# First tile list spread over a turn, the last group's routing put beside the first expert tiles, second tile list two turns later

## The reference

```python
h = h + retention(layernorm(h))              # block A: 8 heads, complex q k v, decay mask, gate
x = layernorm(h)                             # block B: softmax attention, 8 heads
t = layernorm(x + attention(x)) * g + b      # input of block C
probs = softmax(t @ gate_W + gate_b)         # block C: 8 experts, one per token
idx, gw = argmax(probs), max(probs)
out = gelu(t @ W1[idx] + b1[idx]) @ W2[idx] + b2[idx]
return h + out * gw
```

## Time and profile before

| | |
|---|---|
| median of 3 runs | 1406.74 us (1406.08 to 1408.68) |
| the profiled execution's own time | 1403.12 us |
| its span | 1401.3 us |
| TensorE busy | 1349.5 us, 96% |
| VectorE busy | 1010.8 us, 72% |
| ScalarE busy | 718.5 us, 51% |
| GpSimd busy | 407.1 us, 29% |

### The profile page before, as it was taken

The page is one execution under the profiler, slowest core; times in us unless marked ns, Lnnn a source line. Parts: engine busy times, 40 slices in busy tenths (PEclk is TensorE's granted clock), DMA queues, the critical chain, the costliest instruction groups (busy, mean ns, idle before and its releaser), DMA issues.

```text
span 1401.3 us, 40349 instructions
## 1 busy us (share of the span) xinstructions
PE 1349.5 (96%) x14878; PEld 989.6 (71%) x14879; DVE 1010.8 (72%) x2331; ACT 718.5 (51%) x1630; POOL 407.1 (29%) x268
## 2 busy tenths in 40 slices
PE   7899999999999999999999999999999876999998
PEld 5566666666666666666666666666666545899998
DVE  2677777777777777777777777777777865766665
ACT  2255555555555555555555555555555535456655
POOL 0002222222222222222222222222222224656666
PEclk9999999999999999999999999999999979899999
DMA  9322222222222222322232223222221002343332
GB/s 388 139 73 78 84 84 83 84 84 84 84 85 84 84 84 85 84 85 85 84 84 84 83 83 84 84 83 78 79 78 37 14 14 52 93 126 102 105 102 67
DMA packets 95130, 124.61 MB, mean 89 GB/s; under 512 B 56619, under 2 KB 77149, under 8 KB 94592
## 3 DMA queue, kind: packets, MB, share of 16 engines
q1 hardware_dynamic: 38400, 102.47, 22.8%
q0 software_dynamic: 56576, 19.93, 6.8%
HBM read 101.27 MB, written 20.82 MB: 87 GB/s over the span
## 4 chain that ended last, share of the span: by engine, by line
PE 90%; DVE 3%; issue 2%; DMA 2%; POOL 1%; ACT 1%; SPq 0%; DVEq 0%; POOLq 0%; ACTq 0%
PE bank_emb L427 19%; PE bank_z L415 9%; PE bank_s L486 9%; PE bank_y L500 6%; PE bank_s L725 5%; PE bank_x L415 5%; PE bank_s L415 5%; PE bank_x L592 4%; PE bank_s L552 4%; PE bank_y L415 3%; PE bank_z L574 3%; PE bank_x L714 3%; PE bank_y L714 3%; PE bank_x L564 2%; PE bank_s L536 2%
## 5 line engine op out<-in xcount | busy, mean ns | idle before, releaser
L1424 POOL DMA_INDIRECT expert_rows<-row_sb,placei x128 | 276.3, 2158 | 327.7 <-issue 327.7
L427 PE MATMUL bank_emb<-home_x 128*128 128x256 f32 (+1 forms) x1216 | 339.5, 390 | 6.6 <-DMA home_x<-in_x_main 6.6
L427 PEld LDWEIGHTS bank_emb<-home_x 128*128 128x128 f32 (+1 forms) x1216 | 218.1, 191 | 109.5 <-issue 37.5
L1021 DVE TENSOR_TENSOR home_s<-bank_s,con 97x776 f32<-97x776 f32 x256 | 239.6, 957 | 2.6 <-PE bank_s L486 0.9
L1410 POOL COPY h<-txt 128x128 f32<-128x128 f32 x32 | 9.4, 294 | 589.6 <-DVE h L1071 565.6
L1035 DVE TENSOR_REDUCE mx<-bank_s 97x8 f32<-97x776 f32 x128 | 117.7, 961 | 48.0 <-PE bank_s L552 48.0
L1436 POOL DMA_INDIRECT out_tokens<-yo,tok x104 | 121.2, 1165 | 75.1 <-issue 63.8
L486 PE MATMUL bank_s<-qm,xn 32*97 32x452 f32 x1024 | 131.6, 580 | 2.1 <-DVE home_s L1040 1.2
L869 ACT ACTIVATE home_s<-home_s 97x776 f32<-97x776 f32 x128 | 107.8, 842 | 28.4 <-DVE home_s L1040 28.3
L1040 DVE TENSOR_TENSOR home_s<-bank_s,mx 97x776 f32<-97x776 f32 x128 | 117.0, 956 | 0.0
L725 PE MATMUL bank_s<-w2e,home_s 128*128 x832 | 110.2, 276 | 0.0
(11 more groups left out here) (211 smaller groups left out, 2384.6 us busy)
## 6 DMA issues: line engine op xcount, KB each, us to landing
home_x<-in_x_main SPq DMA_DIRECT2D x96, 768.0 KB, 4.4
home_x<-expert_rows SPq DMA_DIRECT2D x104, 129.0 KB
w1e<-in_exp_w SPq DMA_DIRECT2D x1, 2576.0 KB, 11.7
txt<-in_txt_t SPq DMA_DIRECT2D x32, 64.0 KB
w2e<-in_exp_w SPq DMA_DIRECT2D x1, 2048.0 KB, 17.1
expert_rows<-row_sb,placei POOLq DMA_INDIRECT x128, 7.5
out_tokens<-yo,tok POOLq DMA_INDIRECT x104
home_x<-in_x_tail SPq DMA_DIRECT2D x32, 48.0 KB
```

The costliest lines, as they stand in the source:

```text
L427: mm = pe.matmul(banks["emb"][:, 0:NPG], wtok[0:k, c, :], x_sb[0:k, c, :], start=(c == 0), stop=(c == KC - 1))
L1021: ins = dve.tensor_tensor(sm[:, k % 2, 2 * h:2 * h + 2, :], pair(h), decay, ALU.mult)
L1424: pool.indirect_dma_start(out=rows[:, :], out_offset=bass.IndirectOffsetOnAxis(ap=placei[:, k, c:c + 1], axis=0), in_=row_sb[:, k, c, E:E ...
```

## The change

Three things are edited.

1. `first_list` becomes a generator. Its steps are no longer run in one piece at the end of turn 31; in turn 32 VectorE runs one of them after each of its `at` steps (not after the `but_last` ones). `first_list_copy` moves from the end of turn 32 to behind VectorE's fourth step of turn 33.
2. Of the last group, `c_var`, `c_rows`, `c_rank`, `c_row_copy`, `c_exp`, `c_normal`, `c_affine`, all routing steps and the scatter leave the first stage (`but_last`) and stand in the expert stage by hand: `c_var` ahead of the first hidden product, `c_normal` and `c_affine` behind the second `tile_in`, `c_rows` behind the first output product, the rest one or two small steps after a tile, and the scatter on GpSimd between tiles 11 and 12. ScalarE switches its activation table to the one with Exp and back after tile 7. Five of the last group's bank uses get banks s2 and s3, which the tiles don't use.
3. The second list's steps follow behind those, so its product and copy come after expert turn 3, which was turn 1; turns 2 and 3 are written out and the loops start at turn 4.

```diff
-BANK_OF = {use: bank for use, bank, _ in USES}
+LAST_GROUP = {"B.wo": "s3", "C.var2": "s2", "C.rows0": "s3", "C.rows1": "s2", "C.rank": "s3"}
+BANK_OF = {(g, use): LAST_GROUP.get(use, bank) if g == NG - 1 else bank
+           for use, bank, _ in USES for g in range(NG)}
...
+def but_last(step, g, *args, **kw):
+    if g < NG - 1:
+        at(step, g, *args, **kw)
...
@@ TensorE: c_var, c_rows, c_rank of the turns are but_last @@
-            def turn(n, last=False):
+            def turn(n, last=False, beside=None):
...
                     output(n, s, e)
+                    if beside:
+                        next(beside, None)
+
+            def last_rows():
+                c_rows(NG - 1, 1)
+                c_rows(NG - 1, 0)
+                for _ in range(6):
+                    yield
+                c_rank(NG - 1)
 
             pe.wait_ge(s_list, 1)
             pe.wait_ge(s_ew, 32)
-            for bank in ("z", "x", "y", "s0", "s1"):
+            for bank in ("z", "x", "y"):
                 free(pe, bank)
             tile_t(0, 0)
             tile_t(0, 1)
+            c_var(NG - 1)
             hidden(0, 0)
-            turn(0)
+            for bank in ("s0", "s1"):
+                free(pe, bank)
+            turn(0, beside=last_rows())
             turn(1)
+            turn(2)
+            turn(3)
             second_list()
-            with pe.Fori(2, TURNS1) as n:
+            with pe.Fori(4, TURNS1) as n:
...
@@ ScalarE: c_row_copy and c_exp of the turns are but_last @@
-            for s in range(SLOTS):
+            hidden(0, 0)
+            hidden(0, 1)
+            c_row_copy(NG - 1, 1)
+            c_row_copy(NG - 1, 0)
+            for s in range(2, SLOTS):
                 hidden(0, s)
+            act.preload_act_table_set("natural_log_exp_and_others")
+            c_exp(NG - 1)
+            act.preload_act_table(ACT.Gelu_apprx_tanh)
             with act.Fori(1, TURNS) as n:
...
@@ VectorE: first_list yields after each step @@
+            first, after = first_list(), [0]
+
+            def at(step, g, *args, **kw):
+
+                if 0 <= g < NG:
+                    step(g, *args, **kw)
+                    if i == LISTED:
+                        next(first, None)
+                    if i == LISTED + 1:
+                        after[0] += 1
+                        if after[0] == 4:
+                            first_list_copy()
...
@@ c_normal, c_affine, logits ... place_index of the turns are but_last @@
-                if i == LISTED - 1:
-                    first_list()
                 if i == LISTED:
-                    first_list_copy()
+                    for _ in first:
+                        pass
...
+            def last_rows():
+                g = NG - 1
+                yield
+                yield
+                logits(g)
+                logit_max(g)
+                yield
+                logit_shift(g)
+                top(g)
+                yield
+                top_index(g)
+                first_top(g)
+                yield
+                one_hot(g)
+                yield
+                yield
+                place_all(g)
+                run_on(g)
+                yield
+                place_chosen(g)
+                yield
+                exp_sum(g)
+                gate_weight(g)
+                yield
+                place_sum(g)
+                yield
+                place_index(g)
+                yield
+                yield from second_list()
+
             tile_in(0, 0)
             tile_in(0, 1)
-            second = second_list()
-            turn(0, beside=second)
-            turn(1, beside=second)
+            c_normal(NG - 1)
+            c_affine(NG - 1)
+            rest = last_rows()
+            turn(0, beside=rest)
+            turn(1, beside=rest)
+            turn(2, beside=rest)
+            turn(3, beside=rest)
             second_list_copy()
-            with dve.Fori(2, TURNS1 - 1) as n:
+            with dve.Fori(4, TURNS1 - 1) as n:
...
@@ GpSimd @@
-                at(scatter, i - 4)
+                but_last(scatter, i - 4)
...
+            for s in range(SLOTS):
+                send(0, s)
+            for s in range(4):
+                send(1, s)
+            scatter(NG - 1)
+            for s in range(4, SLOTS):
+                send(1, s)
+            with pool.Fori(2, TURNS) as n:
                 for s in range(SLOTS):
+                    send(n, s)
```

More of the change, by code:

```diff
@@ L287, in full, with done, drain @@
         def full(eng, g, name):
-            eng.wait_ge(filled[BANK_OF[name]], COUNT[g, name])
-            return banks[BANK_OF[name].split()[0]]
+            eng.wait_ge(filled[BANK_OF[g, name]], COUNT[g, name])
+            return banks[BANK_OF[g, name].split()[0]]
         def read(eng, g, name):
-            eng.wait_ge(drained[BANK_OF[name]], COUNT[g, name])
-        def done(ins, name):
-            ins.then_inc(filled[BANK_OF[name]], 1)
-        def drain(ins, name):
-            ins.then_inc(drained[BANK_OF[name]], 1)
+            eng.wait_ge(drained[BANK_OF[g, name]], COUNT[g, name])
+        def done(ins, g, name):
+            ins.then_inc(filled[BANK_OF[g, name]], 1)
+        def drain(ins, g, name):
+            ins.then_inc(drained[BANK_OF[g, name]], 1)
         def scattered(eng, n):
@@ L410, in use @@
                     pe.wait_ge(drained[bank], n)
-                return banks[BANK_OF[name].split()[0]]
+                return banks[BANK_OF[g, name].split()[0]]
             def product(g, name, lhs, rhs):
                 ps = use(g, name)
-                done(pe.matmul(ps[:, 0:N], lhs, rhs, start=True, stop=True), name)
+                done(pe.matmul(ps[:, 0:N], lhs, rhs, start=True, stop=True), g, name)
             def embed(g, c0, c1):
@@ L488, in a_scores @@
                     if r % 2:
-                        done(mm, name)
+                        done(mm, g, name)
             def a_mix(g, k):
-                ps = use(g, "A.y") if k == 0 else banks[BANK_OF["A.y"]]
+                ps = use(g, "A.y") if k == 0 else banks[BANK_OF[g, "A.y"]]
                 for h in range(2):
@@ L503, in a_mix @@
                 if k == 3:
-                    done(mm, "A.y")
+                    done(mm, g, "A.y")
                 else:
@@ L564, in b_probs_t @@
                     mm = pe.transpose(ps[0:S, t], prob[:, k, r, t], const("ident")[0:S, 0:S])
-                done(mm, name)
+                done(mm, g, name)
             def b_sums(g, k):
-                ps = use(g, "B.den") if k == 0 else banks[BANK_OF["B.den"]]
+                ps = use(g, "B.den") if k == 0 else banks[BANK_OF[g, "B.den"]]
                 for r in range(4):
@@ L577, in b_sums @@
                 if k == 1:
-                    done(mm, "B.den")
+                    done(mm, g, "B.den")
             def b_mix(g, k):
@@ L594, in b_mix @@
                 if k == 1:
-                    done(mm, "B.o")
+                    done(mm, g, "B.o")
             def b_wo(g):
@@ L620, in c_rows @@
                                    start=True, stop=True)
-                done(mm, f"C.rows{half}")
+                done(mm, g, f"C.rows{half}")
             def c_rank(g):
@@ L632, in c_rank @@
                                    start=False, stop=(c == G - 1), skip_group_check=True)
-                done(mm, "C.rank")
+                done(mm, g, "C.rank")
             def first_list():
@@ L652, in _ @@
                 at(ahead, i + 1, 4, 6)
-                at(c_var, i - 3)
+                but_last(c_var, i - 3)
                 at(ahead, i + 1, 6, 8)
@@ L682, in _ @@
                 at(b_probs_t, i - 2, 0, 0)
-                at(c_rank, i - 3)
+                but_last(c_rank, i - 3)
                 at(b_k, i - 1)
@@ L789, in log @@
                 ps = full(act, g, name)
-                drain(act.activation(dst, ps[:, 0:N], ACT.Ln, bias=const("eps")), name)
+                drain(act.activation(dst, ps[:, 0:N], ACT.Ln, bias=const("eps")), g, name)
             def rstd(g, name, dst, s):
@@ L840, in a_query @@
                 if last:
-                    drain(ins, "A.qr")
+                    drain(ins, g, "A.qr")
             def gate_exp(g):
@@ L858, in b_query @@
                 ps = full(act, g, "B.q")
-                drain(act.activation(q2[:], ps[:, 0:N], ACT.Identity, bias=bq4[:], scale=0.25), "B.q")
+                drain(act.activation(q2[:], ps[:, 0:N], ACT.Identity, bias=bq4[:], scale=0.25), g, "B.q")
             def b_value_rows(g):
@@ L873, in b_probs_copy @@
                 ps = full(act, g, name)
-                drain(act.copy(pt[:, k, r, :], ps[0:S, 0:4 * S]), name)
+                drain(act.copy(pt[:, k, r, :], ps[0:S, 0:4 * S]), g, name)
             def sums_log(g):
                 ps = full(act, g, "B.den")
-                drain(act.activation(rden[:], ps[:, 0:N], ACT.Ln), "B.den")
+                drain(act.activation(rden[:], ps[:, 0:N], ACT.Ln), g, "B.den")
             def sums_reciprocal(g):
```

(8 more changed lines are left out.)

97 lines of the change are left out of this document (55 added, 42 removed).

## The result

| | median us | range, runs |
|---|---|---|
| before, beside the changed kernel | 1406.16 | 1404.66 to 1408.68, 7 |
| changed | 1401.29 | 1400.33 to 1403.71, 7 |
| ratio | 0.9965 | 95% interval 0.9956 to 0.9975 |

The kernel became faster by 4.9 us. Forecast were 13.1, and 1401.29 lies above the range. The profiled execution took 1402.45 us (span 1400.6), against 1403.12 (span 1401.3): a smaller difference than that of the medians, since the one of before was a quick one and the one of after is not.

A forecast was written before the change was run, and what follows sets the result against it. TensorE was taken as the bound nearly everywhere, except a hole in slices 33 to 35. Gains of 6.5 (first list) and 6.6 (last group's move, net) sum to 13.1, from 1406.74 to 1393.6, called 1394; range 1389.5 to 1400.

The forecast's parts named there:

- Part 1: Turn 32: first list's block on VectorE spread among other steps, ending TensorE's idle stretch; gain 6.5 us, bounds 3 and 8.
- the half clock kept for mix and `a_yvar`: Turn 32: the clock stays low for these two products, giving 6.2 us instead of 7.7 at full clock throughout.
- The 0.6 ahead of `a_out`: Turn 32: `a_out` no longer held by other steps' slow products, 0.8 us, less 0.2 for two list steps.
- Part 2: Last group to tile 8: first hidden product 8.9 us earlier, 0.3 more gained by tile 8.
- Part 3: Expert tiles: cost of the last group's work now beside them, 2.6 us, bounds 1.1 to 4.4.
- The prediction's own sign that its costs beside the tiles are wrong: Expert tiles: over 5 us more from first to last hidden product; about 2 us more was expected.
- `c_rank`: Behind tile 6: its five small matmuls cost TensorE 0.4 us (0.2 to 0.7).
- The table switch: ScalarE behind tile 7: two table loads and `c_exp` make TensorE wait 1.0 us (0.5 to 2.0).
- the rival with a dear switch: ScalarE's table loads cost more than their row, 2.6 us more for two switches; 1396.2 us, chance 0.10.
- The scatter ... TensorE loses 0 to 1.8; I take 1.0: Expert tiles: GpSimd's four descriptor writings stop VectorE's weight copies; TensorE loses 1.0 us, bounds 0 to 1.8.
- The reading that a copy stops whenever a writing runs: VectorE: a weight copy starting during a GpSimd descriptor writing stops until it ends, 1.66 us against 0.49.
- The rival of the output writes: Tile 20: output writes queue behind the scatter's, 2.3 us late, copies meeting back-to-back sends another 2; 1397.9 us, chance 0.06.

The follow-up runs named there:

- part 1 alone: Kernel before plus only the first list's steps spread over turn 32 and its copy moved; 1401.05 against 1405.4 us (0.9969), again 1401.96 against 1404.99 (0.9963).

## Why the prediction was wrong

**Part 1.** Forecast 6.5 us: the mix product 5.6 earlier, the rest behind it, with the half clock kept for mix and `a_yvar`. In the trace mix came 6.2 earlier from the turn's start. The half clock stayed for those two, as taken, and `c_var` and the product after it ran at full clock (0.92 and 0.89 us instead of 1.66 and 1.63). The 0.6 ahead of `a_out` didn't come (7.18 us from mix to it, before 7.08), and 5.9 were left at the Wo product. Right in mechanism and nearly in size. The 1.46 us by which turn 32 began late are outside the sum. In the medians part 1 alone gave 3.0 and 4.4. The trace of the second, its slowest execution (1405.38), lost 2.5 more between Wo and the first hidden product (14.58 instead of 12.08) and the 3.9 of tiles 6 to 9; what the other executions lost isn't shown.

**Part 2.** Forecast: Wo to first hidden product 3.1 us instead of 12.1, and 17.4 from there to tile 8. Measured in the first trace 4.61, with a weight copy that met the scatter of group 30 and took 1.87 us, and 17.82. So the gain at tile 8, forecast as 15.7, was 11.7 there: 1.5 of the shortfall is the late start of turn 32, 0.6 the list, 1.4 the gap behind Wo, 0.5 the first tiles. But that trace was the odd one. In all six other traces at the 1405 level that have the move, the two are 2.95 and 16.8 us; at the 1385 level the changed kernel has 2.98 and 16.81. Part 2 was right, and a little too low.

**Part 3, the step that failed.** Forecast 2.6 us, bounds 1.1 to 4.4 (its terms add up to 0.9 and 4.7); measured 11.0, and 11.6 in the second trace. The prediction's own sign that its costs beside the tiles are wrong, over 5 us more from the first to the last hidden product, came: 210.95 against 199.76. `c_rank`, still ahead of tile 8, took 0.16 of its 0.4. The table switch took 1.33 of its 1.0; the rival with a dear switch is refuted, since removing both loads gave back 1.3 to 1.4 us, not 3.6. (The Trainium skill, "ScalarE: Activation LUTs", What ACT_TABLE_LOAD costs, adds about 1380 ns of drain to a load; this case's loads take the 1.28 us that it gives, but the next activation starts 0.02 us behind.) The step that failed is "The scatter ... TensorE loses 0 to 1.8; I take 1.0". I priced it by one mechanism, the weight copies stopped by descriptor writing. That one cost 2.3, over its bound: copies of 0.69 to 1.11 us held the tiles at the scatter's period of 2.45 four times over. (The Trainium skill, "SBUF — State Buffer", Who interferes with whom, on the exclusive lock of VectorE's and GpSimd's port pair: the copy of 8.01 us beside GpSimd's fills agrees in that it waits to the end, here of all five fills.) The reading that a copy stops whenever a writing runs was too wide, too: in the trace of before one that starts 0.5 us into the writing of 1193.69 to 1196.00 isn't stopped:

```profile
1194.21 0.49 DVE L1360 COPY home_x<-w1e 128x644 f32 x1
```

The second price of the same scatter, the hole of 7.6 us behind it, was in no term. The rival of the output writes had the right place, but not what it priced: 1397.9 by a late write and copies among the sends. With an eighth of their rows the hole is there all the same; that their number has a part in it is open.

**The check on it.** The second trace of the changed kernel at the 1405 level (1403.02 us) against that of before: 5.7 gained at the Wo product from the start of turn 32, 9.1 in the gap behind it, 0.8 up to tile 8, 11.6 lost behind it, together 4.1; its medians say 3.8. In the forecast's own terms, 1.0 for the scatter was wrong by 8.9 us: 13.1 - 8.9 = 4.2. That this lies near the 4.9 measured is in part luck, since the pair of traces that 9.9 comes from differs by only 0.7 us of span. At the 1385 level tiles 16 to 24 lose 2.8, and the changed kernel gained 12.3 us (7 to 15 by its interval) with 13.1 forecast. That fits, but there is no trace of before at that level, so the terms weren't measured there one by one.

**Could the trace of before have shown it?** In part. ScalarE's `pt` copy at the same point of three turns in the changed kernel (this code is that of before), the first turn without a scatter in it, the others with one:

```profile
102.66 0.48 ACT L897 COPY pt<-bank_x 97x388 f32<-97x388 f32 x1 [1.83 <-PE bank_x L573]
...
138.22 0.48 ACT L897 COPY pt<-bank_x 97x388 f32<-97x388 f32 x1 [2.69 <-PE bank_x L573]
...
173.78 0.48 ACT L897 COPY pt<-bank_x 97x388 f32<-97x388 f32 x1 [2.68 <-PE bank_x L573]
```

The wait is about 0.86 longer as soon as there is a scatter (the first is issued at 131.60), in each of 28 turns; in the trace of before the same copy waits 2.67. What TensorE shows in it is matmuls that don't arrive: in the turn without scatter the 64 products of line 601 come as one group of 1.53 us, and in the next one they are broken:

```profile
98.95 1.53 PE L601 MATMUL bank_x<-pt,vp 97*32 97x97 f32 x64
...
133.83 1.26 PE L601 MATMUL bank_x<-pt,vp 97*32 97x97 f32 x45
...
135.44 0.61 PE L601 MATMUL bank_x<-pt,vp 97*32 97x97 f32 x17 [0.35 <-issue]
```

At the 1385 level the wait is 1.83 again in most turns, with the scatter still there:

```profile
451.57 0.48 ACT L897 COPY pt<-bank_x 97x388 f32<-97x388 f32 x1 [1.83 <-PE bank_x L573]
```

Over the 28 turns the wait is longer than 1.83 by 23.7 us in all at the 1405 level, and by 4.3 at the 1385 level, where 20 of the 28 are near 1.83. The difference is 19.4, and by 19.4 the stretch itself is shorter (102.66 to 1098.23, and 102.72 to 1078.86). That is nearly the whole distance of the two levels. So what tells them apart is a wait in the turns that have a scatter. It could be read before the change, though not that it would be 7 us beside tiles. That the scatter makes the wait rests on one turn without a scatter in each trace.

**Open.** Why an engine waits behind a scatter is not shown: the waits are labelled "issue" or "remote", in the middle of code whose operands are ready, and engines that share no data with the scatter have them. A supply of instructions or of semaphore writes that is held up by the scatter's transfers would look so, but no run here tells these apart. Nor is it shown whether the scatter does it alone: behind the same four DMAs of the kernel before there is no hole. What makes the level isn't known either.

## What to carry to other kernels

A burst of DMAs that GpSimd writes can have two prices beside a bound engine. One is the copies that its descriptor writing stops, 2.3 us here. The other is waits of all engines behind it, 3 to 10 us after the last one was written and 7.6 us long here. The second has no row with the DMA's name; look for it by comparing a period that has such a DMA with the same period without one. It isn't the burst's alone: in the kernel before the same burst, ahead of the first output writes, cost no such wait. Where a burst is moved in front of writes that will queue behind it, try it spread out as well (here tiles 16 to 32 then lost 6.8 instead of 9.7 us, which the times couldn't tell apart). And measure at more than one time: the same change gave 0.992 at one level and 0.9965 at the other.

## What the runs showed that was not expected

The same program took about 1405 us in some sets of runs and 1385 in others, at the same granted clock (0.99 in both), and the turns that differ are those with a scatter. A hole of 7.5 to 7.6 us came in four different kernels 19.8 us behind the first scatter DMA's start, to within 0.05 us, though not in the second trace of the changed kernel. And a VectorE copy that takes 0.48 us alone stood for 8.01 us while GpSimd filled tiles, and the clock was granted at 0.50 to TensorE behind the wait that this made:

```profile
1203.00:1206.00 3.00, 3.00 (x16) 3.00 (x16) 1.34 (x6) 1.14 (x4) 1.81 (x2) 0.50 0.35 111
```
